# Dispatch stage of a graph network with a soft mixture of experts: logits made one slot tile further ahead of the products, and the column maxima turned and sent in front of the last but one product

## Chip, cores and metric

The kernel runs on one core of a Trainium2 chip. The metric is the device time of one execution in microseconds; the time shown for the kernel before is the median of three runs.

## What is computed

Two graph attention layers over 1250 nodes come first, then a layer norm and a soft mixture of experts. The change lies in the first half of that mixture. Cut to what matters (one batch, N = 1250 nodes, D = 768, 4 experts of 1024 slots, hidden width 384):

```python
logits = jnp.einsum('bnd,esd->bnes', x, phi)
dispatch = jax.nn.softmax(logits, axis=1)                      # over the nodes
combine = jax.nn.softmax(logits.reshape(B, N, E * S), axis=-1) # over all slots
slots = jnp.einsum('bnd,bnes->besd', x, dispatch)
h = jax.nn.gelu(jnp.einsum('besd,edh->besh', slots, w1) + b1[None, :, None, :])
y = jnp.einsum('besh,ehd->besd', h, w2) + b2[None, :, None, :]
out = jnp.einsum('besd,bnes->bnd', y, combine)
```

## The kernel before

The program is a row of stages, each a block that all engines enter and leave together. The one changed is `dispatch`. It goes over ST = 32 slot tiles of 128 slots each. TensorE does two pieces of work for a tile s:

- **L(s), the logits**: phi tile s times the normed inputs, 128 slots by 1250 nodes, as 6 x 3 chunks of three float16 matmuls (high and low halves, `split_product`, lines 102 to 104), 54 matmuls in all. They go into the PSUM banks `lps[s % 2]`, of which there are two sets (`even` and `odd`).
- **P(s), the product**: the turned softmax weights `pt` of tile s times `xw` (inputs times w1, made earlier), 10 x 3 = 30 matmuls of 384 columns into `hp`.

Between the two, for the same tile: ScalarE copies the logits to `lg` (L1721); VectorE takes their maximum `top` (L1787), its negative `neg` (L1790), and the running maximum over all tiles (L1793, `running_max`, which the combining softmax needs); ScalarE makes `p = exp` (L1728) and its float16 high half `pn_hi` (L1733); VectorE makes the low half `pn_lo` (L1805); SyncE turns both halves by DMA into `pt` (L1656). `pt` has one buffer, so the turn of tile s waits until P(s-1) is done (`h_done`).

After P(s), VectorE and ScalarE do its gelu: VectorE `g` (L1764), three more operations (L1769, L1771, L1774), ScalarE tanh `th` (L1708), VectorE L1778, ScalarE `hid_hi` (L1712), VectorE `hid_lo` (L1781).

Each engine has its own function `step(s)`, and `rolled` runs it for s = -1 to 33, the steps 3 to 30 as a hardware loop of pairs. The work of an engine in a step is in the order in which it is written. In one step s of ScalarE and VectorE that is: phi tile s+1 to float16 (`ph_hi` L1699, `ph_lo` L1754), then the gelu of tile s-2, then everything for the logits of tile s. TensorE's step s is L(s), then P(s-1). SyncE's step s loads phi tile s+2, stores `lg`, and turns tile s.

The last tile goes another way (`logits_end`, s = 32). Its weights `p` are turned by TensorE, ten transposes into `tp` (L1829), ScalarE and VectorE copy them to `pt_hi` (L1694) and `pt_lo` (L1745), and P(31) waits for `pt_lo`. The running maximum is turned too, ten transposes into `lp` (L1836); VectorE reduces it to `top_col` (L1750); a last transpose (L1850), placed half way into P(31), makes a row of it, which ScalarE copies to `top_row` (L1703) and SyncE writes out and reads back as `slots_top` for all partitions (L1668, L1670).

The next stage, `combine`, starts with a subtraction of `slots_top` on VectorE (L1995), then exp, two halves, and TensorE (L2076).

Of the kernel before, what the change touches and what calls it, by code (L numbers as in the profile page):

```python
# [27 lines left out]
ALU = mybir.AluOpType  # L28
ACT = mybir.ActivationFunctionType
AX_X = mybir.AxisListType.X  # L30
ds = bass.ds

P = 128
N = 1250
NT = -(-N // P)
NP = NT * P
# [13 lines left out]
ST = EXPERTS * SLOTS // P  # L50
# [37 lines left out]
S_PROB = 4096.0  # L88
# [4 lines left out]
def at_least(eng, sem, value):  # L93

    if not isinstance(value, int) or value > 0:
        eng.wait_ge(sem, value)


def split_product(eng, out, lhs, rhs, first, last):

    (lh, ll), (rh, rl) = lhs, rhs
    eng.matmul(out, lh, rh, start=first, stop=False, skip_group_check=True)  # L102
    eng.matmul(out, lh, rl, start=False, stop=False, skip_group_check=True)  # L103
    return eng.matmul(out, ll, rh, start=False, stop=last, skip_group_check=True)  # L104
# [1475 lines left out]
def dispatch(nc, mem, sem, banks, const, x2t, xw, phi, fb1, running_max, hid, logits, slots_top, max_rows,  # L1580
# [5 lines left out]
    p = mem("p", [P, NP], F32)  # L1586
    pt = [mem(f"pt_{q}", [P, NT, P], F16) for q in ("hi", "lo")]
    pn = [mem(f"pn_{q}", [P, NP], F16) for q in ("hi", "lo")]
    bias = mem("bias", [P, EXPERTS * HID], F32)
# [7 lines left out]
    in_bias, zeroed, max_set, max_ready = (  # L1597
        sem("di_in_bias"), sem("di_zeroed"), sem("di_max_set"), sem("di_max"))
    lg_ready = sem("di_lg")
# [8 lines left out]
    max_turned, max_col, max_turned2, max_row, row_kept, in_top = (  # L1608
        sem("di_mt"), sem("di_mc"), sem("di_mt2"), sem("di_mr"), sem("di_row_kept"), sem("di_in_top"))
    top_col = mem("top_col", [P, NT], F32)  # L1610
    top_row = mem("top_row", [NT, P], F32)
    top = mem("top", [P, 2], F32)

    with nc.Block() as block:
# [3 lines left out]
        lps = [even, odd]  # L1618
        tp, lp = even, odd

        def valid(s):
            return not isinstance(s, int) or 0 <= s < ST
# [12 lines left out]
        def logits_end(s):  # L1635
            return isinstance(s, int) and s == ST
# [50 lines left out]
        @block.scalar  # L1687
        def _(eng):
            def step(s, u):
                w = (u + 1) % 2  # L1690
                if logits_end(s):
                    eng.wait_ge(turned_ready, 1)
                    eng.wait_ge(h_done, ST - 1)
                    eng.activation(pt[0][:, :, :].rearrange("p t n -> p (t n)"), tp[:, 0:NP],  # L1694
                                   ACT.Copy, scale=S_PROB).then_inc(pt_hi, 1)
                if more_phi(s):
                    eng.wait_ge(in_phi[w], 16 * ((s + 1 - w) // 2 + 1))
                    at_least(eng, l_done, s)
                    eng.activation(ph[0][:, w, :, :], phf[:, w, :, :], ACT.Copy, scale=S_WEIGHT)\  # L1699
                       .then_inc(ph_hi, 1)  # L1700
                if logits_end(s):
                    eng.wait_ge(max_turned2, 1)
                    eng.activation(top_row[:, :], lp[0:NT, NP:NP + P], ACT.Copy, bias=-math.log(S_PROB))\  # L1703
                       .then_inc(max_row, 1)
                if here(s - 2):
                    eng.wait_ge(gel, 4 * (s - 1))
                    at_least(eng, hid_hi, s - 2)
                    eng.activation(th[:, :], g2[:, :], ACT.Tanh, scale=0.7978845608028654)\  # L1708
                       .then_inc(th_ready, 1)
                if here(s - 2):  # L1710
                    eng.wait_ge(twice, s - 1)
                    eng.activation(hid[0][:, ds(s - 2, 1), 0:HID], g1[:, :], ACT.Copy, scale=S_ACT / 2)\  # L1712
                       .then_inc(hid_hi, 1)
                if valid(s):
                    eng.wait_ge(l_done, s + 1)

                    at_least(eng, max_ready, s - 1)
                    at_least(eng, top_ready, s - 1)
                    at_least(eng, p_ready, s - 1)
                    at_least(eng, kept[u], 16 * ((s - u) // 2))  # L1720
                    eng.activation(lg[:, u, :], lps[u][:, 0:N], ACT.Copy, scale=1.0 / (S_NORM * S_WEIGHT))\  # L1721
                       .then_inc(lg_ready, 1)
                if valid(s):
                    eng.wait_ge(neg_ready, s + 1)
                    at_least(eng, pn_hi, s)
                    at_least(eng, pn_lo, s)
                    at_least(eng, inv_ready, 2 * (s - 1))
                    eng.activation(p[:, 0:N], lg[:, u, :], ACT.Exp, bias=neg[:, u:u + 1],  # L1728
                                   accum_out=den[:, u:u + 1]).then_inc(p_ready, 1)
                if here(s):  # L1730
                    eng.wait_ge(p_ready, s + 1)
                    at_least(eng, in_pt[0], 16 * s)
                    eng.activation(pn[0][:, 0:N], p[:, 0:N], ACT.Copy, scale=S_PROB).then_inc(pn_hi, 1)  # L1733
            run(eng, step)

        @block.vector
        def _(eng):
# [3 lines left out]
            def step(s, u):  # L1741
                w = (u + 1) % 2
                if logits_end(s):
                    eng.wait_ge(pt_hi, 1)
                    eng.scalar_tensor_tensor(pt[1][:, :, :].rearrange("p t n -> p (t n)"), tp[:, 0:NP],  # L1745
                                             S_PROB, pt[0][:, :, :].rearrange("p t n -> p (t n)"),
                                             ALU.mult, ALU.subtract).then_inc(pt_lo, 1)
                if logits_end(s):
                    eng.wait_ge(max_turned, 1)
                    eng.tensor_reduce(top_col[:, :], lp[:, 0:NP].rearrange("p (t n) -> p t n", t=NT),  # L1750
                                      AX_X, ALU.max).then_inc(max_col, 1)
                if more_phi(s):
                    eng.wait_ge(ph_hi, s + 2)
                    eng.scalar_tensor_tensor(ph[1][:, w, :, :].rearrange("p k n -> p (k n)"),  # L1754
# [3 lines left out]
                if valid(s - 2):  # L1758

                    k = s - 2  # L1760
# [14 lines left out]
                if here(s - 2):  # L1775
                    k = s - 2
# [35 lines left out]
        @block.tensor  # L1812
        def _(eng):
            def step(s, u):
                w = (u + 1) % 2
                if valid(s) and not (isinstance(s, int) and s == 0):
                    eng.wait_ge(ph_lo, s + 1)
                    at_least(eng, lg_ready, s - 1)
                    for k in range(KD):
                        for a, n in CHUNKS:  # L1820
                            mm = split_product(eng, lps[u][:, a:a + n], [q[:, u, k, :] for q in ph],
                                               [q[:, k, a:a + n] for q in x2t],
                                               k == 0, k == KD - 1)
                    mm.then_inc(l_done, 1)
                if logits_end(s):
                    eng.wait_ge(zeroed, 3)
                    eng.wait_ge(p_ready, ST)
                    for t in range(NT):
                        mm = eng.transpose(tp[:, t * P:(t + 1) * P], p[:, t * P:(t + 1) * P],  # L1829
                                           const["ident"][:, :])  # L1830
                    mm.then_inc(turned_ready, 1)
                if logits_end(s):
                    eng.wait_ge(max_ready, ST)
                    eng.wait_ge(lg_ready, ST)
                    for t in range(NT):
                        mm = eng.transpose(lp[:, t * P:(t + 1) * P], running_max[:, t * P:(t + 1) * P],  # L1836
                                           const["ident"][:, :])
                    mm.then_inc(max_turned, 1)
                if valid(s - 1):
                    expert = (s - 1) // STE  # L1840
                    if logits_end(s):
                        eng.wait_ge(pt_lo, 1)
                    else:
                        for arrived in in_pt:
                            eng.wait_ge(arrived, 16 * s)
                    at_least(eng, gel, 4 * (s - 3) + 1)
                    for t in range(NT):
                        if logits_end(s) and t == NT // 2:
                            eng.wait_ge(max_col, 1)
                            eng.transpose(lp[0:NT, NP:NP + P], top_col[:, :], const["ident"][:, :])\  # L1850
                               .then_inc(max_turned2, 1)
                        mm = split_product(eng, hp[:, w, 0:HID], [q[:, t, :] for q in pt],
                                           [q[:, t, ds(expert * HID, HID)] for q in xw],
                                           t == 0, t == NT - 1)
                    mm.then_inc(h_done, 1)
            run(eng, step)
# [389 lines left out]
```

## Time and profile before

| | us |
|---|---|
| median of three runs | 1707.67 (1706.31 to 1708.2) |
| profiled execution, its own time | 1710.9 |
| span of that execution | 1709.1 |
| TensorE busy over the span | 1557.3 (91%) |
| VectorE busy | 1102.0 (64%) |
| ScalarE busy | 846.2 (50%) |
| GpSimd busy | 272.4 (16%) |

Start times of rows count from the start of the span. A matmul's row shows a modelled end that overlaps the next one; the distance from one start to the next is what a matmul costs in a run of them. The number in square brackets behind a row is the idle time of its engine before it, with what ended it. L numbers are lines of the kernel before.

### The profile page before, as it was taken

The numbers are of one execution on the slowest core, as the hardware profiler recorded it, in microseconds if no ns is written. First come the engines' busy times: TensorE is split into PE (matmuls) and PEld (weight loads), VectorE is DVE, ScalarE is ACT, GpSimd is POOL, SyncE is SP. The second block draws the span as 40 slices with busy tenths as digits, with TensorE's granted clock in tenths as the row PEclk, the third lists the DMA queues.
The fourth block names the chain that finished last, engine by engine and source line by source line (L and its number), as shares of the span: only waits on it lengthen the run. The fifth ranks groups of instructions, "written<-read, shape, count | busy, mean of one in ns | idle before, by whom it ended". The sixth has DMA issues, their size and how long they took to land. (4 is left out here: it accounts for less than half of the span.)

```text
span 1709.1 us, 24928 instructions
## 1 busy us (share of the span) xinstructions
PE 1557.3 (91%) x8615; PEld 882.5 (52%) x8615; DVE 1102.0 (64%) x1810; ACT 846.2 (50%) x1322; POOL 272.4 (16%) x120
## 2 busy tenths in 40 slices
PE   6896666599999989999999899999999989999999
PEld 3442332366666545555554455555555545555555
DVE  7989999699999937553332456666666666766200
ACT  3159999688888827421111333333333335656000
POOL 1000000687877707000000000000000000000000
PEclk9998889699999989999999999999999998999999
DMA  4000100023232336441210544444444446783211
GB/s 180 19 29 27 44 19 11 4 34 37 32 50 34 22 81 164 103 134 56 56 47 28 133 116 117 116 117 117 119 119 119 119 124 206 214 214 98 74 56 53
DMA packets 204683, 146.91 MB, mean 86 GB/s; under 512 B 171758, under 2 KB 173768, under 8 KB 204464
## 3 DMA queue, kind: packets, MB, share of 16 engines
q1 hardware_dynamic: 204592, 145.75, 33.8%
q8 instruction: 51, 0.84, 0.3%
q14 instruction: 40, 0.33, 0.1%
HBM read 78.70 MB, written 28.35 MB: 63 GB/s over the span
## 5 line engine op out<-in xcount | busy, mean ns | idle before, releaser
L1006 POOL TENSOR_TENSOR base<-s_row,ln_c 128x1250 f32<-128x1250 f32 x80 | 227.6, 2847 | 58.5 <-DVE top L1068 56.2
L102 PE MATMUL sl_di<-x2t_hi,ph_hi 128*128 128x512 f16 (+1 forms) x576 | 195.5, 339 | 0.3 <-PEq L1226 0.3
L104 PE MATMUL sl_di<-x2t_hi,ph_lo 128*128 128x512 f16 (+1 forms) x576 | 195.5, 339 | 0.0
L103 PE MATMUL sl_di<-x2t_lo,ph_hi 128*128 128x512 f16 (+1 forms) x576 | 195.5, 339 | 0.0
L1155 PE MATMUL at_o<-pt,h 128*128 128x384 f32 (+1 forms) x480 | 188.2, 530 | 1.9 <-DVE h L1103 1.9
L901 PE MATMUL fs<-one_src,one_dst 128*128 128x512 f16 x720 | 120.4, 324 | 63.7 <-ACT one_dst L812 54.6
L1134 PE MATMUL at_t<-ident,q 128*128 128x128 f32 x800 | 108.1, 285 | 36.7 <-ACT q L1040 35.9
L1134 PEld LDWEIGHTS at_t<-ident,q 128*128 128x128 f32 x800 | 93.6, 146 | 79.7 <-ACT q L1040 69.7
L647 DVE TENSOR_SCALAR one_src<-iota,src,worth 128x625 f16<-128x625 f16 x360 | 131.9, 442 | 3.2 <-PE fs L901 2.1
L1016 ACT ACTIVATE at_r<-s_row,nad 128x1250 f32<-128x1250 f32 x80 | 104.5, 1307 | 37.8 <-DVE top L1068 37.1
L901 PEld LDWEIGHTS fs<-one_src,one_dst 128*128 128x128 f16 x720 | 56.8, 106 | 126.9 <-ACT one_dst L812 73.2
L1068 DVE CUSTOM_DVE_ANT_0 q<-at_r,base 128x1250 f32<-128x1250 f32 x80 | 116.2, 1453 | 5.5 <-POOL base L1006 3.6
L1077 DVE COPY pt<-at_t 128x512 f32<-128x512 f32 x160 | 103.2, 685 | 23.0 <-PE at_t L1134 22.6
L1155 PEld LDWEIGHTS at_o<-pt,h 128*128 128x128 f32 x480 | 86.8, 194 | 57.5 <-issue 27.6
L2076 PE MATMUL co_c<-hid_hi,ps_hi 128*128 128x385 f16 x320 | 105.9, 331 | 8.7 <-DVE ps_lo L2010 8.7
L102 PE MATMUL sl_di<-xw,pt_hi 128*128 (+1 forms) x320 | 105.3, 329 | 7.4 <-DMA pt_lo<-pn_lo 5.7
L1787 DVE TENSOR_REDUCE top<-lg 128x1 f32<-128x1250 f32 x32 | 46.5, 1454 | 98.4 <-ACT lg L1721 86.0
L1040 ACT ACTIVATE q<-q,neg_top 128x1250 f32<-128x1250 f32 x80 | 105.9, 1323 | 0.1
L2080 PE MATMUL co_c<-hid_hi,ps_lo 128*128 128x385 f16 x320 | 105.4, 329 | 0.0
L103 PE MATMUL sl_di<-xw,pt_hi 128*128 (+1 forms) x320 | 105.3, 329 | 0.0
L104 PE MATMUL sl_di<-xw,pt_lo 128*128 (+1 forms) x320 | 105.3, 329 | 0.0
L2078 PE MATMUL co_c<-hid_lo,ps_hi 128*128 128x384 f16 x320 | 105.0, 328 | 0.0
(270 smaller groups left out, 3137.9 us busy)
## 6 DMA issues: line engine op xcount, KB each, us to landing
logits_t<-lg SPq DMA_DIRECT2D x32, 625.0 KB, 3.2
phf<-in_phi SPq DMA_DIRECT2D x32, 384.0 KB, 3.5
logits_in<-logits_t SPq DMA_DIRECT2D x16, 640.0 KB, 5.5
logits_in<-logits_t SPq DMA_DIRECT2D x16, 610.0 KB, 5.3
w2f<-in_w2t SPq DMA_DIRECT2D x16, 384.0 KB, 3.4
s_row<-a_rows SPq DMA_DIRECT2D x9, 640.0 KB, 6.5
ew1f<-in_fw SPq DMA_DIRECT2D x6, 768.0 KB, 5.3
wf<-in_fw SPq DMA_DIRECT2D x12, 384.0 KB, 6.2
```

Of the source, the lines that this page charges most:

```text
L102: eng.matmul(out, lh, rh, start=first, stop=False, skip_group_check=True)
L103: eng.matmul(out, lh, rl, start=False, stop=False, skip_group_check=True)
L104: return eng.matmul(out, ll, rh, start=False, stop=last, skip_group_check=True)
L647: eng.tensor_scalar(one_src[:, place(b, i), 0:HALF], const["iota"][:, 0:HALF], src[:, ds(col, 1)], worth[:, ds(col, 1)], ALU.is_equal, ALU ...
L901: mm = eng.matmul(counts(g)[:, a:a + n], one_dst[:, place(b, i), :], one_src[:, place(b, i), a:a + n], start=False, stop=b == PIECES - 1 a ...
L1006: eng.tensor_tensor(base[:, k % 2, 0:N], s_row[:, head % 2, 0:N], ln_c[:, j, 0:N], ALU.add)\
L1040: eng.activation(q[:, k % RING, 0:N], q[:, k % RING, 0:N], ACT.Exp, bias=neg_top[:, k:k + 1], accum_out=den[:, k:k + 1]).then_inc(p_ready, 1)
L1068: eng.tensor_tensor_reduce(q[:, k % RING, 0:N], rp[:, 0:N], base[:, k % 2, 0:N], 1.0, -MASK / 2, ALU.add, ALU.max, top[:, k:k + 1]).then_i ...
L1134: mm = eng.transpose(tp[:, t * P:(t + 1) * P], q[:, k % RING, t * P:(t + 1) * P], const["ident"][:, :])
L1155: mm = eng.matmul(op[:, g % 2, 0:n * P], h[:, head, t, :], pt[:, a:a + n, t, :], start=t == 0, stop=t == NT - 1, skip_group_check=True)
L2076: eng.matmul(cp[:, bank, 0:HID + 1], high, hid[0][:, slot, 0:HID + 1], start=begin, stop=False, skip_group_check=True)
L2080: mm = eng.matmul(cp[:, bank, 0:HID + 1], low, hid[0][:, slot, 0:HID + 1], start=False, stop=end, skip_group_check=True)
```

## The change

TensorE's step s now does L(s+1) and then P(s-1), where it did L(s) and then P(s-1). L(s+1) has the wait for the phi half of its tile (`ph_lo`) and for the copy out of the same banks (`lg_ready`), each shifted by one. The waits, the order and the steps of the other engines for tiles before the last stay as they are. At the end, the ten transposes of `running_max` stand in step 31, in front of P(30); the transpose of `top_col` comes right behind P(30), and the ten transposes of `p` behind that. ScalarE's copy of the row of maxima and VectorE's reduction to `top_col` move in front of the copies of `pt`.

```diff
             def step(s, u):
                 w = (u + 1) % 2
-                if valid(s) and not (isinstance(s, int) and s == 0):
-                    eng.wait_ge(ph_lo, s + 1)
-                    at_least(eng, lg_ready, s - 1)
+                if valid(s + 1) and not (isinstance(s, int) and s < 0):
+                    eng.wait_ge(ph_lo, s + 2)
+                    at_least(eng, lg_ready, s)
                     for k in range(KD):
                         for a, n in CHUNKS:
-                            mm = split_product(eng, lps[u][:, a:a + n], [q[:, u, k, :] for q in ph],
+                            mm = split_product(eng, lps[w][:, a:a + n], [q[:, w, k, :] for q in ph],
                                                [q[:, k, a:a + n] for q in x2t],
                                                k == 0, k == KD - 1)
                     mm.then_inc(l_done, 1)
+                if isinstance(s, int) and s == ST - 1:
+                    eng.wait_ge(max_ready, ST)
+                    eng.wait_ge(lg_ready, ST)
+                    for t in range(NT):
+                        mm = eng.transpose(lp[:, t * P:(t + 1) * P], running_max[:, t * P:(t + 1) * P],
+                                           const["ident"][:, :])
+                    mm.then_inc(max_turned, 1)
                 if logits_end(s):
+                    eng.wait_ge(max_col, 1)
+                    eng.transpose(lp[0:NT, NP:NP + P], top_col[:, :], const["ident"][:, :])\
+                       .then_inc(max_turned2, 1)
                     eng.wait_ge(zeroed, 3)
                     eng.wait_ge(p_ready, ST)
                     for t in range(NT):
                         mm = eng.transpose(tp[:, t * P:(t + 1) * P], p[:, t * P:(t + 1) * P],
                                            const["ident"][:, :])
                     mm.then_inc(turned_ready, 1)
-                if logits_end(s):
-                    eng.wait_ge(max_ready, ST)
-                    eng.wait_ge(lg_ready, ST)
-                    for t in range(NT):
-                        mm = eng.transpose(lp[:, t * P:(t + 1) * P], running_max[:, t * P:(t + 1) * P],
-                                           const["ident"][:, :])
-                    mm.then_inc(max_turned, 1)
...
                     for t in range(NT):
-                        if logits_end(s) and t == NT // 2:
-                            eng.wait_ge(max_col, 1)
-                            eng.transpose(lp[0:NT, NP:NP + P], top_col[:, :], const["ident"][:, :])\
-                               .then_inc(max_turned2, 1)
                         mm = split_product(eng, hp[:, w, 0:HID], [q[:, t, :] for q in pt],
```

The order of the instructions, at the places that matter. First TensorE at the start of the stage, before: rows with `x2t` are logits, rows with `xw` are products.

```order
L103 MATMUL sl_di<-x2t_lo_14167,ph_hi_14177 128x226
L104 MATMUL sl_di<-x2t_hi_14166,ph_lo_14178 128x226
L102 MATMUL sl_di<-xw_90,pt_hi_16839 128x384
...
L104 MATMUL sl_di<-xw_90,pt_lo_16840 128x384
L102 MATMUL sl_di<-x2t_hi_14166,ph_hi_14177 128x512
```

and the same place in the changed kernel:

```order
L103 MATMUL sl_di<-x2t_lo_14167,ph_hi_14177 128x226
L104 MATMUL sl_di<-x2t_hi_14166,ph_lo_14178 128x226
L102 MATMUL sl_di<-x2t_hi_14166,ph_hi_14177 128x512
...
L104 MATMUL sl_di<-x2t_hi_14166,ph_lo_14178 128x226
L102 MATMUL sl_di<-xw_90,pt_hi_16839 128x384
```

Behind the last matmul of L(1) stood the first of P(0); now the 54 matmuls of L(2) stand between them.

Second, TensorE at the end of the stage, before, from the end of L(31) to the start of P(31) and into it:

```order
L104 MATMUL sl_di<-x2t_hi_14166,ph_lo_14178 128x226
L102 MATMUL sl_di<-xw_90,pt_hi_16839 128x384
...
L104 MATMUL sl_di<-xw_90,pt_lo_16840 128x384
L1829 MATMUL sl_di<-ident_49,p_16838 128x128 x10
L1836 MATMUL sl_di<-ident_49,running_max_16831 128x128 x10
L102 MATMUL sl_di<-xw_90,pt_hi_16839 128x384
...
L1850 MATMUL sl_di<-ident_49,top_col_16851 10x128
```

and in the changed kernel, from the end of P(29), which is now the piece behind L(31), to the start of P(31):

```order
L104 MATMUL sl_di<-xw_90,pt_lo_16840 128x384
L1829 MATMUL sl_di<-ident_49,running_max_16831 128x128 x10
L102 MATMUL sl_di<-xw_90,pt_hi_16839 128x384
...
L104 MATMUL sl_di<-xw_90,pt_lo_16840 128x384
L1834 MATMUL sl_di<-ident_49,top_col_16851 10x128
L1839 MATMUL sl_di<-ident_49,p_16838 128x128 x10
L102 MATMUL sl_di<-xw_90,pt_hi_16839 128x384
```

The transposes of `running_max` stood behind P(30) and stand in front of it now.

Third, ScalarE in the changed kernel, from the gelu of tile 29 (tanh and `hid_hi`) over the logits of tile 31 to the gelu of tile 30:

```order
L1708 ACTIVATE th_16850<-g_118_16849 128x384
L1712 ACTIVATE hid_hi_16832<-g_117_16848 128x384
L1721 ACTIVATE lg_16837<-sl_di 128x1250
L1728 ACTIVATE p_16838,den_16845<-lg_16837,neg_16844 128x1250
L1693 ACTIVATE top_row_16852<-sl_di 10x128
L1698 ACTIVATE pt_hi_16839<-sl_di 128x1280
L1708 ACTIVATE th_16850<-g_118_16849 128x384
```

Only the two rows behind `p` have changed places; `lg` of tile 31 stands behind `th` and `hid_hi` of tile 29, as before.

## Rows read from the trace of the kernel before

**Rows 1.** The page: its first line.

```profile
span 1709.1 us, 24928 instructions
```

**Rows 2.** Waits of TensorE, 936 to 1440 us: us in total, times, longest.

```profile
PE co_c L2076 <- DVE ps_lo L2010: 8.7, 1, 8.7
PE sl_di L102 <- DMA pt_lo<-pn_lo: 5.7, 1, 5.7
PE sl_di L102 <- DVE pt_lo L1745: 1.8, 1, 1.8
```

**Rows 3.** Busy time by engine in two stretches, x instructions; at the end granted clock, DMA share, GB/s.

```profile
958.00:960.00 2.00, 2.00 (x7) 0.91 (x6) 1.94 (x2) 0.87 (x2) 0.00 (x0) 0.50 0.55 225
980.00:1376.00 396.00, 396.00 (x2313) 225.50 (x2312) 241.23 (x359) 154.05 (x191) 0.00 (x0) 1.00 0.45 117
```

**Rows 4.** Timeline, VectorE and TensorE, start of the stage.

```profile
952.78 0.95 DVE L1754 SCALAR_TENSOR_TENSOR ph_lo<-phf,ph_hi 128x768 f16<-128x768 f32 x1
956.54 0.48 PE L102 MATMUL sl_di<-xw,pt_hi 128*128 128x384 f16 x1 [5.67 <-DMA pt_lo<-pn_lo]
963.79 0.38 PE L102 MATMUL sl_di<-x2t_hi,ph_hi 128*128 128x512 f16 x1
```

**Rows 5.** Timeline, TensorE, first stage: two idle times of 3 us.

```profile
189.86 5.05 PE L901 MATMUL fs<-one_src,one_dst 128*128 128x512 f16 x24 [3.03 <-ACT one_dst L812]
266.82 1.78 PE L901 MATMUL fs<-one_src,one_dst 128*128 128x512 f16 x12 [3.03 <-ACT one_dst L812]
```

**Rows 6.** Timeline of the loop, one tile: SyncE, VectorE, ScalarE, TensorE.

```profile
1196.80 1.39 SPq L1656 DMA_TRANSPOSE pt_lo<-pn_lo  x1
1197.56 0.61 DVE L1764 SCALAR_TENSOR_TENSOR g<-sl_di,inv,bias 128x384 f32<-128x384 f32 x1
1201.02 0.52 ACT L1712 ACTIVATE hid_hi<-g 128x384 f32 x1 [0.71 <-DVE g L1778]
1203.46 0.33 PE L102 MATMUL sl_di<-xw,pt_hi 128*128 x1
1203.75 1.21 ACT L1721 ACTIVATE lg<-sl_di 128x1250 f32<-128x1250 f32 x1 [2.20 <-PE sl_di L104]
1204.99 1.45 DVE L1787 TENSOR_REDUCE top<-lg 128x1 f32<-128x1250 f32 x1 [2.71 <-ACT lg L1721]
1206.55 1.45 DVE L1793 TENSOR_TENSOR running_max<-running_max,lg 128x1250 f32<-128x1250 f32 x1
1208.29 1.25 ACT L1733 ACTIVATE pn_hi<-p 128x1250 f16<-128x1250 f32 x1
1209.65 1.46 DVE L1805 SCALAR_TENSOR_TENSOR pn_lo<-p,pn_hi 128x1250 f16<-128x1250 f32 x1 [1.00 <-ACT pn_hi L1733]
1211.03 0.95 DVE L1754 SCALAR_TENSOR_TENSOR ph_lo<-phf,ph_hi 128x768 f16<-128x768 f32 x1
```

**Rows 7.** DMA issues of the page: KB each, median us to landing.

```profile
phf<-in_phi SPq DMA_DIRECT2D x32, 384.0 KB, 3.5
```

**Rows 8.** Timeline, end of the stage: TensorE, ScalarE, VectorE, SyncE.

```profile
1390.47 0.33 PE L102 MATMUL sl_di<-xw,pt_hi 128*128 128x384 f16 x1
1395.34 1.26 PE L1829 MATMUL sl_di<-ident,p 128*128 128x128 f32 x10
1396.44 1.25 PE L1836 MATMUL sl_di<-ident,running_max 128*128 128x128 f32 x10
1399.45 0.34 PE L102 MATMUL sl_di<-xw,pt_hi 128*128 128x384 f16 x1 [1.76 <-DVE pt_lo L1745]
1402.21 0.27 ACT L1703 ACTIVATE top_row<-sl_di 10x128 f32<-10x128 f32 x1 [4.34 <-PE sl_di L1850]
1405.31 0.62 DVE L1764 SCALAR_TENSOR_TENSOR g<-sl_di,inv,bias 128x384 f32<-128x384 f32 x1
1406.53 19.68 SPq L1922 DMA_DIRECT2D logits_in<-logits_t  x7
1407.62 2.89 DVE L1995 TENSOR_TENSOR p<-logits_in,slots_top 128x1280 f32<-128x1280 f32 x2 [1.70 <-DMA slots_top<-row_max_rows]
```

More of the change, by code:

```diff
@@ L1691, in step @@
                 if logits_end(s):
+                    eng.wait_ge(max_turned2, 1)
+                    eng.activation(top_row[:, :], lp[0:NT, NP:NP + P], ACT.Copy, bias=-math.log(S_PROB))\
+                       .then_inc(max_row, 1)
+                if logits_end(s):
                     eng.wait_ge(turned_ready, 1)
@@ L1700, in step @@
                        .then_inc(ph_hi, 1)
-                if logits_end(s):
-                    eng.wait_ge(max_turned2, 1)
-                    eng.activation(top_row[:, :], lp[0:NT, NP:NP + P], ACT.Copy, bias=-math.log(S_PROB))\
-                       .then_inc(max_row, 1)
                 if here(s - 2):
@@ L1743, in step @@
                 if logits_end(s):
+                    eng.wait_ge(max_turned, 1)
+                    eng.tensor_reduce(top_col[:, :], lp[:, 0:NP].rearrange("p (t n) -> p t n", t=NT),
+                                      AX_X, ALU.max).then_inc(max_col, 1)
+                if logits_end(s):
                     eng.wait_ge(pt_hi, 1)
@@ L1747, in step @@
                                              ALU.mult, ALU.subtract).then_inc(pt_lo, 1)
[L1748 to L1751, printed above, removed]
                 if more_phi(s):
@@ L1831, in step @@
                     mm.then_inc(turned_ready, 1)
-                if logits_end(s):
-                    eng.wait_ge(max_ready, ST)
-                    eng.wait_ge(lg_ready, ST)
-                    for t in range(NT):
-                        mm = eng.transpose(lp[:, t * P:(t + 1) * P], running_max[:, t * P:(t + 1) * P],
-                                           const["ident"][:, :])
-                    mm.then_inc(max_turned, 1)
                 if valid(s - 1):
```

## The prediction

> **What bounds the kernel now.** I read the waits of TensorE over the dispatch stage first, then the busy time in its loop, then the timelines at its start and its end. The waits show three idle stretches and no more: 5.7 us at the start, before the first product; 1.8 us near the end, before the last product; 8.7 us behind it, before the first matmul of the next stage [rows 2]. Between 980 and 1376 us TensorE is busy for 396.00 of 396.00 us at a granted clock of 1.00 [rows 3]. It does 84 matmuls a tile (54 of logits, 30 of a product), so a tile costs 396.00 / 2313 x 84 = 14.38 us. A product takes 1395.34 - 1390.47 = 4.87 us [rows 8], so a tile's logits take 9.51 us. In the loop only TensorE counts, and the change gives it the same matmuls in another order. The loop can't become faster, only slower; what can be gained or lost otherwise lies in the stage's two ends, against about 16 us of idle time in all.
>
> The sum is made against the profiled execution, 1710.9 us (span 1709.1 [rows 1]); it stands 3.2 us above the median of the runs, 1707.67, and I carry the difference over to the median. A measurement of this kernel can tell about 0.2%, 3.4 us, from no change.
>
> **The start.** Before, TensorE went from L(1) to P(0), and P(0) waited 5.67 us for its turned weights [rows 4]. L(1) so ended at 956.54 - 5.67 = 950.87. Now L(2) comes first. It needs `ph_lo` of tile 2, which was done at 952.78 + 0.95 = 953.73 [rows 4] and hangs on nothing that the change touches, and the copy of L(0) out of its banks, long done. So L(2) starts at about 953.78, and the idle time shrinks from 5.67 to 2.91 us: a gain of 2.76. By the end of L(2), 963.3, the weights of tile 0, there at 956.5, cost P(0) nothing.
>
> The clock belongs to this. Behind the 5.67 us of idle time it was granted at 0.50, the lower of the two levels (1.2 GHz) [rows 3], and P(0) took 963.79 - 956.54 = 7.25 us instead of 4.87 [rows 4], 2.38 more. What follows 2.91 us of idle time the stage doesn't show. The nearest rows are in the first stage: behind 3.03 us of idle time, 24 matmuls took 5.05 us in one place, where 12 took 1.78 behind the same idle time in another, so two times 12 would be about 3.6 to 3.7 [rows 5]. One wait cost 1.4 us, the other nothing. The bounds for L(2) are 0 and 2.38; I take 1.3, since the 3.03 us rows are the nearest by far. Of the 2.38 us, 1.1 are saved. The start gains 2.8 + 1.1 = 3.9 us, with bounds of 2.8 and 5.1.
>
> **The loop.** TensorE now does L(s+1), P(s-1) in step s, and VectorE and ScalarE still do the gelu of tile s-2 before the logits of tile s. This makes a new circle. From the end of P(s-2), TensorE has L(s+1) and P(s-1) to do, 14.38 us, and then wants phi tile s+2 in halves. In that time the other engines must do the gelu, the logits and the phi halves, one behind the other. By the loop's rows [rows 6]: a consumer starts 0.29 us after the end of TensorE's work (1203.46 to 1203.75); `g` to the end of `hid_hi` 3.98 (1197.56 to 1201.54); `lg` to `top` 1.24; `top` to `pn_hi` 3.30; `pn_hi` to `pn_lo` 1.36; `pn_lo` to the end of `ph_lo` 2.33. Together 12.50 us, so 1.88 us are left. Until now this chain had the whole wait for `lg` in it (2.20 us of ScalarE's idle time) and nobody noticed.
>
> The DMAs on SyncE's queue hold up too. The turn of tile s still waits for P(s-1), and now L(s+2) alone, 9.51 us, covers it. The low half was issued at 1196.80 and the product that needs it began at 1203.46 without a wait, so it took at most 6.66 us [rows 6]; issued some 1.5 us behind P(s-1), it is there at 8.2. The load of the next phi tile comes 1.4 us behind and lands in 3.5 us [rows 7], at about 6.5, and is wanted after `pn_hi`, beyond 8.8. The loop costs nothing; what covers the chain is 1.88 us of slack, and any stretch beyond it is paid in each of some 28 tiles.
>
> **The end.** Let E be the end of P(29). In the changed kernel it follows L(31), so at E exactly the work is done that was done before at 1390.47, the end of L(31): all but P(30) and P(31) [rows 8]. From there the first subtraction of the next stage was 1407.62 - 1390.47 = 17.15 us away.
>
> Now TensorE comes to the transposes of `running_max`, which need the logits of tile 31. But `lg` of tile 31 stands on ScalarE behind `th` and `hid_hi` of tile 29, and these need P(29), that is E. By the durations above `hid_hi` ends at E + 0.29 + 3.98 = 4.27, `top` starts at 5.51, `running_max` 1.56 later at 7.07 and ends at E + 8.5 [rows 6]. TensorE stands still for 8.3 us, a new wait, with P(30) queued behind it though its weights are ready. Then: transposes 1.10 (1395.34 to 1396.44) and P(30) 4.87 [rows 8], with 2.4 more for the clock, priced by P(0) behind its 5.67 us: E + 16.9. `top_col` is ready by then. Transposes of `p` from E + 17.0; P(31) came 1399.45 - 1395.34 = 4.11 after their start, through `pt_hi` and `pt_lo` [rows 8]: E + 21.1. The idle time in it is 2.9 us instead of 1.76, since the other transposes no longer fill it, and its clock is priced as at the start, 1.3, with bounds of 0 and 2.4. P(31) ends at E + 21.1 + 4.87 + 1.3 = 27.3, the `g` behind it at + 0.29 + 0.62 = 28.2, and the stage changes in 0.6 (1405.31 + 0.62 to 1406.53) [rows 8]: first subtraction at E + 28.8.
>
> The maxima do go out earlier. `top_row` is made at E + 17.2, and 5.41 us later (1402.21 to 1407.62) [rows 8] they are there, at E + 22.6, well before the stage ends. That takes away the wait of 1.70 us that the first subtraction had, and all of it is in the sum already. The end costs 28.8 - 17.15 = 11.7 us, bounds 10.3 (both waits short of a further clock loss) and 13.2.
>
> **Sum.** 11.7 - 3.9 = 7.8 us: 1718.7 against the profiled execution, **1715.5** against the median. Its own bounds are 10.3 - 5.1 = 5.2 and 13.2 - 2.8 = 10.4, so 1712.9 to 1718.1.
>
> On the clock the Trainium skill would have me leave these terms out: "For modeling, the ramp penalty is <1% of a typical kernel span; don't fit to a specific cold count" (TensorE: Matmul & The Clock Gate, section "What's actually happening"). The trace agrees as to the share (2.38 of 1709 us is 0.14%), but the whole effect here is no larger. Without any clock term the start gains 2.8 and the end costs 7.9, so by that rule the sum would be 5.1 us, 1712.8.
>
> **The rivals.**
>
> *The clock holds through the short waits and the long one.* Then the start gains 5.1 and the end costs 11.7 - 2.4 - 1.3 = 8.0: 2.9 us slower, 1710.6, which counts as no change. For it: one of two waits of 3.03 us cost nothing [rows 5]. Against it: 5.67 us of idle time did bring the lower level [rows 3, 4], and the new one is 8.3 us. I give it 0.09.
>
> *The maxima's wait is covered, and the change is faster.* If `lg` of tile 31 could start as L(31) ends, `running_max` would be done 0.29 + 1.24 + 1.56 + 1.45 = 4.54 us later [rows 6], inside P(29)'s 4.87. No new wait; the transposes of the maxima take 1.10, P(30) 4.87, P(31) starts at E + 10.2, the first subtraction comes at E + 10.2 + 4.87 + 0.29 + 0.62 + 0.6 = 16.6 where it was 17.15: 0.6 gained at the end, 3.9 at the start, 4.5 in all, 1703.2. It decides on one point: whether the gelu of tile 29 has left ScalarE before L(31) ends. In the order `th` and `hid_hi` of tile 29 stand in front of `lg`, and P(29) stands behind L(31), which speaks against it. The extra clock loss at P(31), 1.3, would leave 3.2 of it, too little to tell. I give it 0.08, and put 0.05 of that on faster by over 0.2%.
>
> *The loop becomes bound by the new circle.* If the chain of 12.50 us were stretched beyond 14.38, by a turn of the weights or a phi load that lands late, or by slower VectorE and ScalarE while transfers bunch behind P(s-1), each 0.5 us over it costs 0.5 x 28 = 14 us: 1729.5 in all. Against it is the slack of 1.88 us and VectorE's busy time of 241.23 / 396 x 14.38 = 8.8 us a tile [rows 3]. I give it 0.08.
>
> **How the numbers follow.** My forecast has 0.75. Slower by over 0.2%: 0.75 + 0.08 = 0.83. Within: 0.09 + 0.03 = 0.12. Faster: 0.05. The range takes in the forecast's own bounds, a measurement's spread of about 0.7 us above, and the first rival in its upper half: 1709.8 to 1718.8. It leaves out the loop's rival, the faster one, and the tails of the rest, together under 0.2.
>
> **What would show it.** Right: a wait of TensorE of about 8 us in front of the ten transposes of `running_max`, ended by VectorE's running maximum; one of about 2.9 us in front of L(2) and one of the same size in front of P(31); no other between them; 7 us instead of 8.7 in front of the next stage. The first subtraction no longer waits for `slots_top`. Wrong: TensorE waits in the loop for `ph_lo` or `pt` (then the circle decides); no wait before those transposes (then the order on ScalarE was misread); or waits as forecast but products at full clock behind them (then only the clock terms fall).

## The result, and the profile after

The changed kernel takes 1711.62 us (median of 15 runs, 1709.81 to 1713.11), the kernel before 1706.45 (15 runs, 1705.52 to 1708.36). The ratio is 1.0029 with a 95% interval of 1.0021 to 1.0036: about 5 us slower. The profiled execution spans 1710.3 us against 1709.1 [rows 1]. These two spans differ by 1.2 us only, since the stages in front, which the change doesn't touch, ended 3.5 us earlier in the second profile (the dispatch stage begins at 937.7 us there, at 941.2 before). So the length of the stage itself is compared below, from its first logits matmul to the first matmul of the next stage: 472.1 us before, 478.0 after, 5.9 more. What follows takes 295.8 and 294.6 us, since the next stage's first matmuls run at the lower clock for a shorter time (the first 20 take 5.8 us before and 4.6 after), so 4.7 us are left of the 5.9.

The waits of TensorE from 936 to 1440 us in the changed kernel (us in total, times, longest), the same view as [rows 2]:

```profile
PE sl_di L1829 <- DVE running_max L1793: 8.1, 1, 8.1
PE co_c L2075 <- DVE ps_lo L2009: 7.0, 1, 7.0
PE sl_di L102 <- DVE pt_lo L1749: 2.9, 1, 2.9
PE sl_di L102 <- DVE ph_lo L1754: 2.1, 1, 2.1
```

The wait of 5.7 us for the first weights is gone, one of 2.1 us for `ph_lo` has come in its place. At the end the 1.8 us in front of P(31) have become 2.9, the 8.7 us in front of the next stage 7.0, and the largest is new: 8.1 us in front of the transposes of `running_max`. The loop, as in [rows 3]:

```profile
980.00:1376.00 396.00, 396.00 (x2312) 225.51 (x2311) 244.38 (x360) 154.15 (x195) 0.00 (x0) 1.00 0.46 118
```

TensorE is busy in all 396.00 us, as before. The start, TensorE's rows where its kind of work changes (answering [rows 4]):

```profile
949.47 0.39 PE L102 MATMUL sl_di<-x2t_hi,ph_hi 128*128 128x512 f16 x1 [2.09 <-DVE ph_lo L1754]
958.99 0.33 PE L102 MATMUL sl_di<-xw,pt_hi 128*128 128x384 f16 x1
963.87 0.38 PE L102 MATMUL sl_di<-x2t_hi,ph_hi 128*128 128x512 f16 x1
```

L(2) begins at 949.47, P(0) at 958.99, and P(0) ends at 963.87 after 4.88 us, at the full clock. The end, by engine: SyncE, ScalarE, VectorE, TensorE, and VectorE again:

```profile
1381.22 1.34 SPq L1656 DMA_TRANSPOSE pt_hi<-pn_hi  x1
1382.61 1.50 SPq L1656 DMA_TRANSPOSE pt_lo<-pn_lo  x1
1384.61 0.52 ACT L1712 ACTIVATE hid_hi<-g 128x384 f16<-128x384 f32 x1 [0.63 <-DVE g L1778]
1385.04 1.19 ACT L1721 ACTIVATE lg<-sl_di 128x1250 f32<-128x1250 f32 x1
1386.27 1.45 DVE L1787 TENSOR_REDUCE top<-lg 128x1 f32<-128x1250 f32 x1 [0.54 <-ACT lg L1721]
1387.83 1.45 DVE L1793 TENSOR_TENSOR running_max<-running_max,lg 128x1250 f32<-128x1250 f32 x1
1389.33 2.40 PE L1829 MATMUL sl_di<-ident,running_max 128*128 128x128 f32 x10 [8.14 <-DVE running_max L1793]
1391.52 0.53 PE L102 MATMUL sl_di<-xw,pt_hi 128*128 128x384 f16 x1
1398.05 0.27 PE L1834 MATMUL sl_di<-ident,top_col 128*10 128x128 f32 x1
1402.27 0.50 PE L102 MATMUL sl_di<-xw,pt_hi 128*128 128x384 f16 x1 [2.86 <-DVE pt_lo L1749]
1408.74 0.62 DVE L1764 SCALAR_TENSOR_TENSOR g<-sl_di,inv,bias 128x384 f32<-128x384 f32 x1 [2.12 <-PE sl_di L104]
1410.08 2.89 DVE L1994 TENSOR_TENSOR p<-logits_in,slots_top 128x1280 f32<-128x1280 f32 x2 [0.71 <-PEq L1614]
```

P(29) ran from 1376.16 to 1381.03, and the turn of tile 30 was issued 0.19 later. `lg` of tile 31 (L1721) follows `hid_hi` of tile 29 on ScalarE, `top` and `running_max` follow it, and TensorE goes on at 1389.33, with the transposes taking 2.19 us instead of 1.10, at the lower clock. TensorE's granted clock in these 2.19 us is 0.50 (columns as in [rows 3]):

```profile
1389.33:1391.52 2.19, 2.19 (x10) 2.13 (x11) 0.32 (x2) 0.04 (x1) 0.00 (x0) 0.50 0.95 310
```

The first subtraction starts right behind the change of stages, no longer behind `slots_top`.

### The profile page after: what moved, and what is told of

Same layout as the page of the kernel before. It is cut to its first block and busy times, and to the rows that moved or that the text cites. A ratio compares the mean times of both kernels' runs of the same rounds, so it can differ in the third digit from the quotient of the medians.

```text
span 1710.3 us, 24928 instructions
## 1 busy us (share of the span) xinstructions
PE 1554.7 (91%) x8615; PEld 882.2 (52%) x8615; DVE 1103.6 (65%) x1810; ACT 843.0 (49%) x1322; POOL 271.4 (16%) x120
## 5 line engine op out<-in xcount | busy, mean ns | idle before, releaser
L1077 DVE COPY pt<-at_t 128x512 f32<-128x512 f32 x160 | 103.2, 685 | 23.0 <-PE at_t L1134 22.6
L1708 ACT ACTIVATE th<-g 128x384 f32<-128x384 f32 x31 | 16.2, 523 | 195.9 <-DVE g L1774 195.9
L807 ACT ACTIVATE apart<-iota,minus_dst 128x128 f16<-128x128 f16 x330 | 102.2, 386 | 5.1 <-issue 2.6
```

## The experiments

The times scatter by more than a single effect is worth. Part of that comes from outside the stage: it begins between 936.2 and 944.0 us in the fourteen profiles, though no edit touches what stands in front. Inside the stage, logits and products at the full clock take 9.51 and 4.87 us in every profile; what varies there without an edit is the arrival of the first load (0.8 us) and the clock behind waits (up to 2.9 us). So each run is read by three lengths from its profile as well: S, the stage (first logits matmul to the first matmul of the next stage); H, from the stage's start to the end of P(0), with 9.51 us for L(2) taken off where it lies in between; and T, from the moment at which all but P(30) and P(31) is done (the end of L(31) before, of P(29) where the logits are ahead) to the first subtraction of the next stage. S, H and T come from one execution each. Times are medians, with the ratio to the kernel before, measured beside it: its median was 1707.70 us beside e1, e2 and e4, 1707.38 beside e5, e10, e11 and e3b, 1707.07 beside e7, e8, e9 and e12, and 1706.75 beside e13. The medians are of 11 or 12 runs, but of 6 for e10, 5 for e12 and 4 for e7, e8 and e9.

| kernel | us | ratio (95%) | S | H | T |
|---|---|---|---|---|---|
| before (beside the change) | 1706.45 | | 472.1 | 22.6 | 17.2 |
| the change | 1711.62 | 1.0029 (1.0021 to 1.0036) | 478.0 | 16.7 | 29.1 |
| e1, start only | 1709.82 | 1.0013 (1.0000 to 1.0026) | 474.1 | 16.6 | 25.1 |
| e4, maxima alone | 1712.21 | 1.0025 (1.0015 to 1.0035) | 477.5 | 22.3 | 22.9 |
| e2, last logits first | 1709.91 | 1.0014 (1.0002 to 1.0026) | 474.1 | 16.5 | 25.2 |
| e10, own buffer | 1713.24 | 1.0039 (1.0026 to 1.0053) | 480.8 | 19.1 | 29.4 |
| e11, both waits off | 1705.60 | 0.9996 (0.9986 to 1.0006) | 470.2 | 19.1 | 18.8 |
| e3b, filled wait | 1712.55 | 1.0030 (1.0018 to 1.0041) | 473.9 | 16.6 | 25.0 |
| e13, the same again | 1710.71 | 1.0023 (1.0014 to 1.0032) | 477.5 | 18.5 | 26.7 |
| e5, before, bias late | 1702.25 | 0.9971 (0.9960 to 0.9982) | 464.9 | 15.7 | 16.9 |
| e12, all three | 1697.93 | 0.9945 (0.9932 to 0.9959) | 463.8 | 14.4 | 17.1 |
| e7, two more operations | 1735.62 | 1.0166 (1.0151 to 1.0182) | 501.4 | | |
| e8, one more | 1716.39 | 1.0055 (1.0040 to 1.0070) | 480.8 | | |
| e9, two more in before | 1728.34 | 1.0121 (1.0106 to 1.0137) | 493.8 | | |

**The halves of the change.** The first takes the end back to the old order in TensorE, ScalarE and VectorE, and leaves the logits ahead; the second takes the logits back (`lps[u]`, `ph_lo >= s + 1`) and leaves the end. Of the first edit the fence shows the condition alone; the order of the transposes and of their copies goes back with it.

```diff
-                if isinstance(s, int) and s == ST - 1:
+                if logits_end(s):
                     eng.wait_ge(max_ready, ST)
                     eng.wait_ge(lg_ready, ST)
```

> The changed kernel with the end of the stage in the old order: the transposes of p and of running_max behind P(30), the one of top_col half way into P(31). Only the logits stay one tile further ahead. Both theories see the start unchanged from the changed kernel (about 5.9 us gained against the kernel before, by its trace: P(0) ended 16.7 us of work and waits after L(1) began instead of 22.6, L(2) left out). Theory (the loss is a wait for the last logits, which stand on ScalarE behind the gelu of tile 29): P(30) now covers most of it; TensorE waits about 3.4 us for p instead of 8.1 for running_max, P(31) begins 12.5 us after the end of P(29), and the row of maxima is late again, so that the first subtraction of the next stage comes at about 21 us where it was 17.2 before and 29.1 in the change. Sum -5.9 + 3.9 = -2.0: about 1704.5 us. Rival (the logits' advance itself costs in the loop or at the end, whatever the place of the maxima): a time at or above that of the changed kernel, 1711.6.

It came out at a ratio of 1.0013 and a stage 2.0 us longer than before, not 2 shorter; neither the theory nor its rival had this. The start's gain is there (H 16.6). But T is 25.1 us where 21 were expected, and TensorE's waits, in the columns of [rows 2], show one that I had not seen:

```profile
PE co_c L2076 <- DVE ps_lo L2010: 8.7, 1, 8.7
PE sl_di L102 <- issue: 5.1, 1, 5.1
PE sl_di L102 <- DVE ph_lo L1754: 2.1, 1, 2.1
PE sl_di L102 <- DVE pt_lo L1745: 1.8, 1, 1.8
```

SyncE's and TensorE's rows at that place suggest what the wait of 5.1 us is for (the runs with a buffer of its own, below, test it):

```profile
1386.11 1.34 SPq L1656 DMA_TRANSPOSE pt_hi<-pn_hi  x1
1387.49 1.50 SPq L1656 DMA_TRANSPOSE pt_lo<-pn_lo  x1
1391.20 0.48 PE L102 MATMUL sl_di<-xw,pt_hi 128*128 128x384 f16 x1 [5.12 <-issue]
```

P(29) ended at 1385.92, the turn of the weights of tile 30 was issued at 1386.11 and 1387.49, and P(30) began at 1391.20. The turn waits for P(29), because `pt` has one buffer. In the loop 9.5 us of logits lie between one product and the next and cover it. At the end of the new order P(29) and P(30) stand next to each other, with no logits left to put between them.

> The other half of the change alone: TensorE's logits in step with the others as before (L(s), then P(s-1)), with the maxima turned in front of P(30) and sent out behind it. Theory: the start is as before (5.7 us of waiting for the weights of tile 0, then a slow product). At the end L(31) stands right in front of the transposes, which wait about 4.5 us for its copy, maximum and running maximum; then 1.1, P(30) 4.9, and P(31) 4.1 us after the transposes of p begin; the first subtraction comes 21.1 us after L(31) plus 0 to 3.7 for the clock, instead of 17.2. Time 1706.5 + 3.9 to + 7.7, about 1711.5. Rival (sending the maxima early pays, and only the logits' advance costs): at or below 1706.5.

As the theory had it: ratio 1.0025, the first subtraction 22.9 us after L(31), a wait of 4.3 us for the running maximum. Maxima sent out early do not pay by themselves. That the other half, e1, costs on its own is shown by its stage of one execution only; its ratio's interval begins at 1.0000.

**The first wait of the end.** Only the last logits step is turned round, on both engines (cut to its core, with comments put in):

```diff
+                if isinstance(s, int) and s == ST - 1:
+                    weights()   # lg and exp (VectorE: maxima) of tile 31
+                    gelu()      # tile 29
+                else:
+                    gelu()
+                    weights()
```

> The changed kernel with one order turned in its last logits step alone: ScalarE's lg and exp of tile 31 and VectorE's maxima of tile 31 stand in front of the gelu of tile 29 instead of behind it. Theory: the wait of 8.1 us in front of the transposes of running_max falls to about 0.4 us, since lg of tile 31 can begin as L(31) ends and P(29) covers it; with it goes the clock loss of 2.7 us behind the wait. The first subtraction comes 17.0 to 18.3 us after P(29), where it was 29.1. Time about 1701.5 us, 10 us below the changed kernel and 5 below the one before. Rival (the wait has another cause, such as the transposes themselves, the copy out of the banks or SyncE's queue): a wait of 5 us or more stays, and the time stays above 1708.

The wait did fall from 8.1 to 0.2 us (the transposes start 5.09 us after P(29) starts, and P(29) lasts 4.88), so the cause of that wait was right. But the time fell only to a ratio of 1.0014, not to the 1701.5 us expected. Behind the transposes TensorE waited again, 3.7 us, until P(30) began 5.26 us after the end of P(29), the same distance as in e1: the turn. Two waits lay one over the other, and the later hid the earlier.

**The second, and both.** The weights of tile 30 get a buffer of their own in the place of the phi tiles, whose last reader is done by then.

```diff
-                    at_least(eng, h_done, s)
+                    late = isinstance(s, int) and s == ST - 2
+                    if late:
+                        eng.wait_ge(ph_lo, ST)
+                    else:
+                        at_least(eng, h_done, s)
...
-                        eng.dma_start_transpose(pt[half][:, :, :], pn[half][:, :]).then_inc(in_pt[half], 16)
+                        eng.dma_start_transpose((own if late else pt)[half][:, :, :], pn[half][:, :])\
+                           .then_inc(in_pt[half], 16)
```

> The changed kernel with a buffer of its own for the turned weights of tile 30 (in the place of the phi tiles, free by then), so that their turn by DMA does not wait for P(29). The two runs before showed P(30) beginning 5.3 us after the end of P(29), as the single buffer's turn landed. Theory (two waits lie over one another at the end: the turn of tile 30, over at 5.3 us, and the running maximum, over at 8.3; only the later counts): no change from the changed kernel, 5.2 us above the kernel before. Rival (the turn costs on its own): 3 us or more below the changed kernel.

The turn of tile 30 is now issued 4.3 and 2.7 us before the end of P(29), instead of 0.2 and 1.6 behind it. T stayed at 29.4 us and the wait in front of the transposes at 8.1, with a ratio of 1.0039. The turn alone is worth nothing while the running maximum comes later.

> Both at once: the own buffer for tile 30, and the logits of tile 31 in front of the gelu of tile 29 on ScalarE and VectorE. Theory (these two waits are the whole of the loss): P(30) follows P(29) with nothing between but 1.1 us of transposes, P(31) begins 10.4 us after the end of P(29), the first subtraction of the next stage comes at about 17 to 18 us where it was 29.1 in the change and 17.2 before; with the start's 5.9 us gained this is 5 to 6 us below the kernel before, and 10 below the changed one. Rival (a third wait lies under them): not below the kernel before.

The waits of this kernel:

```profile
PE co_c L2105 <- DVE ps_lo L2039: 7.1, 1, 7.1
PE sl_di L102 <- DVE ph_lo L1773: 2.9, 1, 2.9
PE sl_di L102 <- DVE pt_lo L1768: 2.9, 1, 2.9
```

Both waits at the end are gone, T fell from 29.1 to 18.8 us, so these two and the clock behind them are the loss. The times bear it out: the ratio is 0.9996 (0.9986 to 1.0006), and the change's 1.0021 to 1.0036 lies above it, while neither edit alone was clear of the change. But this is no difference from before, where 5 to 6 us less were expected. That is the rival's time, though the end of the stage shows no wait beyond those expected. In this execution the stage is 1.9 us shorter than before. The rest of the 5 to 6 us went into the clock, which fell twice behind waits of 2.9 us (L(2) took 11.2 us instead of 9.5, and P(31) and what follows it 13.8 instead of 12.1, 1.7 each), and into a first load that came 0.8 us later than in the change.

**The clock.** 45 matmuls that nobody reads fill the new wait:

```diff
+                    eng.wait_ge(lg_ready, ST - 1)
+                    for _ in range(45):
+                        eng.matmul(tp[:, 0:HID], xw[0][:, 0, 0:P], xw[0][:, 0, 0:HID], start=True, stop=True,
+                                   skip_group_check=True)
                     eng.wait_ge(max_ready, ST)
```

> The changed kernel with 45 matmuls of 384 columns, whose result nobody reads, put into the wait in front of the transposes of running_max (45 x 0.163 = 7.3 us of the 8.1). It prices the clock alone. Theory: the transposes and P(30) take 6.0 us instead of 8.7, and P(31) loses 0 to 1.3; the time falls by 2.7 to 4 us, to 1.2 to 2.5 above the kernel before. Rival (the clock is no part of it, the lost time is all waiting): no change, 5.2 us above the kernel before.

The granted clock of the transposes and P(30) was 1.00 in its profile, and the stage 4.1 us shorter than the changed kernel's, but the median stood 5.2 us above the kernel before. The transposes and P(30), columns as in [rows 3]:

```profile
1393.46:1399.48 6.02, 6.02 (x40) 4.06 (x41) 1.81 (x3) 0.04 (x1) 0.00 (x0) 1.00 0.62 211
```

The same kernel was run once more.

> The kernel of the filled wait once more. Its first run left a contradiction: the stage was 4.1 us shorter in its trace than in the changed kernel's (the clock held for the transposes, P(30) and P(31)), but its times stood as far above the kernel before as the changed kernel's. If the saving is real, the stage is again about 474 us long from the first L(1) matmul to the first matmul of the next stage, against 478.0, and the median stands 1 to 3 us above the kernel before (part of the first result was scatter of the stages in front). If the matmuls cost elsewhere what they save here, the stage is as short again and the median 5 us above again. If the held clock was chance, the stage is 476 to 478.

In both executions the transposes and P(30) took 6.02 us (451.60 to 457.62 and 453.50 to 459.53 us into the stage) against 8.72 in the changed kernel (1389.33 to 1398.05): the clock's price of that wait is 2.7 us in this pair. It is no fixed price: behind the same 8.1 us of waiting the same work took 8.92 us in e10, but 7.62 and 7.69 in e7 and e8, so 1.6 to 2.9 us. Also, the two profiles of the same kernel differ by 3.6 us in S, through the short waits. In the second one, the waits of TensorE and then the busy times from 949.6 to 952.0 us, columns as in [rows 3]:

```profile
PE sl_di L102 <- DVE pt_lo L1749: 2.9, 1, 2.9
PE sl_di L102 <- DVE ph_lo L1754: 2.3, 1, 2.3
949.60:952.00 2.40, 2.40 (x9) 1.11 (x8) 2.06 (x5) 1.93 (x3) 0.00 (x0) 0.55 1.00 203
```

Behind 2.3 us of waiting the granted clock was 0.55; behind 2.1 us in e3b, e1 and the change it stayed full. The medians stand 5.2 and 4.0 us above the kernel before, so the times neither show the saving of 2.7 us nor rule it out: expected were 1.2 to 2.5, and both intervals overlap the change's. The saving rests on part of a profile, the medians on 11 runs each; where the rest goes in the unprofiled runs stays open.

**Is the start's gain the advance's?** The first product of [rows 4] is late since the whole chain in front of it starts late: VectorE waits for a bias that only the gelu reads. The kernel before, VectorE's first row of the stage:

```profile
946.99 1.45 DVE L1787 TENSOR_REDUCE top<-lg 128x1 f32<-128x1250 f32 x1 [12.34 <-DMA bias<-in_fb]
```

That is 5.8 us into the stage; the first gelu begins at 964.00.

```diff
-            eng.wait_ge(in_bias, 16)
             eng.wait_ge(max_set, 1)
...
                     eng.wait_ge(h_done, k + 1)
+                    if isinstance(s, int) and s == 2:
+                        eng.wait_ge(in_bias, 16)
```

> The kernel before, with VectorE's wait for the bias load moved from the start of the stage to the first gelu, the first reader of it. In the trace of before VectorE stood idle until 946.99 for that load, with the first logits copied at 942.4. Theory (the first product's 5.7 us wait, which the logits' advance shortened, goes back to this load): the first maximum comes about 4.5 us earlier, the wait falls to about 1.2 us and the clock is not lost: 6.8 us below the kernel before. Rival (the turn by DMA is the bound, whenever the maximum is made): a wait of 4 us or more stays, and the gain is below 3 us.

VectorE's first row of the stage, now 1.2 us into it, and then TensorE's waits:

```profile
942.98 1.45 DVE L1788 TENSOR_REDUCE top<-lg 128x1 f32<-128x1250 f32 x1 [7.88 <-POOL running_max L1680]
PE co_c L2077 <- DVE ps_lo L2011: 8.4, 1, 8.4
PE sl_di L102 <- DVE pt_lo L1744: 1.8, 1, 1.8
PE sl_di L102 <- DMA pt_lo<-pn_lo: 1.1, 1, 1.1
```

The wait for the first weights fell from 5.7 to 1.1 us, S by 7.2 us, and the time to a ratio of 0.9971: faster than both kernels, without any of the change.

> The changed kernel with both waits at the end taken away (own buffer for tile 30, logits of tile 31 in front of the gelu of tile 29) and the bias load waited for at the first gelu only. Theory: TensorE's wait of 2.1 us in front of L(2) goes too; 2.1 us below the same kernel without the third edit, about 7 to 8 us below the kernel before, and so within 1 us of the kernel before with the bias wait moved and nothing else: then the logits' advance does little but hide that load. Rival (the advance gains something of its own): 3 us or more below that kernel.

This is the fastest kernel of the study, 1697.93 us, 0.55% below the one before. Its stage is 463.8 us long, 1.1 us shorter than e5's, as the theory had it. It is 6.4 us shorter than e11's, though, where 2.1 were expected: the first wait, 2.9 us in e11, is gone, and the clock, which had cost e11 1.7 us twice, held in both places. By the times it stands 9.1 us below its own runs of the kernel before and e5 5.1 us, measured at different times. A profile of each says the advance adds about 1 us to the moved wait, the medians say 4, which would be the rival's case. The two were not measured side by side, so this stays open.

**The circle in the loop.** VectorE's `pn_lo` is computed n times more in each tile (n = 2, 1, and 2 in the kernel before):

```diff
+                    for i in range(n):
+                        eng.scalar_tensor_tensor(pn[1][:, 0:N], p[:, 0:N], S_PROB, pn[0][:, 0:N],
+                                                 ALU.mult, ALU.subtract).then_inc(again, 1)
+                        eng.wait_ge(again, n * s + (i + 1))
```

> The changed kernel with VectorE's low half of the weights computed three times over instead of once, in each tile: two operations of 1.38 us more in the circle from P(s-2) to L(s+2). Theory (the circle of 12.50 us has 1.9 us to spare): 12.50 + 2.76 = 15.3 us, 0.9 to 1.0 over the 14.38 of a tile's matmuls, in some 28 tiles: 25 to 28 us slower, about 1738, and TensorE waits for ph_lo in every tile. Rival (there is no such circle, VectorE has 40% of the loop free): 1712.

```profile
PE sl_di L102 <- DVE ph_lo L1755: 14.0, 26, 0.6
```

1735.62 us, 24.0 above the changed kernel where 25 to 28 were expected, with TensorE waiting for `ph_lo` in each of the 26 tiles of the stretch from 980 to 1376 us. A tile takes 15.09 us there (27 tiles from 979.63 to 1387.13), 0.71 over 14.38. The two operations added 2.99 us (1191.02 to 1194.01), so the circle is 12.1 us and has 2.3 to spare; the working had 12.5 and 1.9.

> The same with one operation more instead of two. Theory: 12.50 + 1.38 = 13.9 us stays below 14.38, no wait in the loop, about 1712 to 1713 (the extra operation may show once at the stage's ends). Rival (the circle is tighter than worked out): some us per ten tiles, 1720 or more.

No wait of TensorE between 980 and 1376 us, and S 2.8 us above the changed kernel's, all at the ends. The time, 1716.39, is higher than the 1712 to 1713 expected. The loop is as the theory had it; what it missed is the start, where TensorE's wait for `ph_lo` is 4.4 us instead of 2.1 and L(2) behind it takes 12.4 us instead of 9.5.

> The kernel before with the same two operations more in each tile. Theory (the advance made the circle; before, P(s-1) came before the logits that the chain follows): no wait of TensorE in the loop, 1706.5 to 1710 (the operations lie once in the path of the first product, 2.8 us). Rival (VectorE is simply too slow with two more, in either order): about 25 us slower, as in the changed kernel.

```profile
PE sl_di L102 <- DMA pt_lo<-pn_lo: 12.1, 23, 0.9
```

Here my theory fell. The kernel before waits in the loop too, for the turned weights, and a tile takes 15.05 us (26 tiles from 988.41 to 1379.81). By the wait's name its chain runs from L(s) over the weights and their turn to P(s), under P(s-1) and L(s+1), and it has 2.99 - 0.67 = 2.3 us to spare. The advance exchanged one circle for another with the same slack, as far as work on VectorE goes. It bought the loop nothing, neither time nor tolerance.

## Why the prediction was right or wrong

The forecast was 1715.5 us in a range of 1709.8 to 1718.8, slower at 0.83. It is slower, by 5.2 us where 7.8 were summed. In the profiles the stage is 5.9 us longer, 2 less than summed, nearly all of it at the start. The sum also ended at the first subtraction of the next stage, and 1.2 us were got back behind that, in the clock of the next stage's first matmuls.

- *The loop costs nothing*: right, 396.00 of 396.00 us busy. The chain of 12.50 us measures 12.1 in the run with two more operations.
- *The start gains 3.9 us*: it gained 22.59 + 9.51 - 26.16 = 5.9. The term for the clock behind the short wait, taken as 1.3, was 0 in this profile. In three others (e10, e11 and e13) the clock did fall there, and L(2) took 11.2 us instead of 9.5, 1.7 more. So 1.3 stands between two outcomes and was met by neither, and that the sum came out near is in part luck. The wait itself was 2.09 us instead of 2.91: the load of the bias came 0.8 us earlier in this execution.
- *The end costs 11.7 us*: it cost 29.05 - 17.15 = 11.9. The new wait was 8.1 us (8.3 forecast), the clock behind it took 8.72 - 5.97 = 2.75 (2.4 taken), P(31) began 4.2 us after the transpose of `top_col` and lost about 1.4 to the clock (1.3 taken). `slots_top` no longer holds anything up, as said. The upper bound, 13.2, doesn't follow from the terms given, which lead to 12.8; nothing hangs on it.
- *"with P(30) queued behind it though its weights are ready"*: wrong. The step that failed is the one on SyncE's queue, where "L(s+2) alone, 9.51 us, covers it" was worked out for the loop and not asked again for tile 30, since no L stands between P(29) and P(30). The turn of tile 30 lands 5.3 us after P(29) (e1, e2). It changed no number of the sum, since the other wait is longer, but it took the ground from the faster rival: with the maxima's wait gone e2 is still slower than before, not 4.5 us faster. Only with the turn's wait gone too does T come near its 16.6 us (e12: 17.1).
- *By the rule quoted from the Trainium skill* (TensorE: Matmul & The Clock Gate, section "What's actually happening"), without clock terms, the sum was 5.1 us, and the medians differ by 5.2. That is not its merit, and the working's remark that the whole effect is no larger than one such term (2.38 us) was wrong, since it summed 7.8. The terms the rule leaves out were 2.4 us of gain at the start and 2.75 and 1.4 of cost at the end in this profile, nearly 2 us net, and the stage shows 5.9. As far as it warns against fixed counts, the runs bear it out, since the same kernel lost its clock behind a wait of about 2 us in one execution and kept it in another.

## What to carry to other kernels

When a piece of work is moved ahead in a pipeline, walk through the last iterations by themselves: what lay between two pieces of work in the loop is missing there, and a single buffer that was covered comes into the open. Where a new wait is found, ask which waits lie under it, since taking it away gives back only the difference to the next one. And before reordering a loop to hide a late start, look at what the first instruction waits for: here a load that nobody needed yet held up the start, and moving its wait gained 6.9 us there (H 22.6 to 15.7), where the reordering gained 5.9.

## What the runs showed of the hardware that was not expected

What a wait costs in TensorE's clock was no fixed amount, even for waits of the same length. Behind waits of 2.85 to 2.87 us in front of P(31) the clock fell in some executions and not in others: from P(31)'s first matmul to the next stage's took 12.1 us in e3b, e4, e7, e8 and e12, and 13.5 to 13.8 in the change, e2, e10, e11 and e13. Of these, e3b and e13 are the same kernel. Nor did the price grow with the wait: of P(0) in the old order it was 2.7 us behind 5.0 us of waiting (e4), 2.4 behind 5.7 (before) and 2.8 behind 8.5 (e9). With the short wait at the start, this lack of a fixed price makes one kernel's stage 473.9 or 477.5 us long in two profiles, 3.6 us or 0.2% of the whole, which is as much as these edits are worth.
